# The first group's variances by adding transfers through DRAM, and x's first columns on SyncE's queue

## What is computed

```
def leaky_relu(x):
    return jnp.maximum(0.05 * x, x)

def layer_norm(x):
    mu = jnp.mean(x, axis=-1, keepdims=True)
    sigma = jnp.sqrt(jnp.mean((x - mu) ** 2, axis=-1, keepdims=True))
    return (x - mu) / sigma
x1, x2 = (x[:, :F], x[:, F:])
h1 = leaky_relu(layer_norm(x1 @ W1.T))      # W1: 256 x 5120
h2 = leaky_relu(layer_norm(x2 @ W1.T))
h1 = leaky_relu(layer_norm(h1 @ W2.T))      # W2: 64 x 256
h2 = leaky_relu(layer_norm(h2 @ W2.T))
h = jnp.concatenate([h1, h2], axis=-1)
h = leaky_relu(layer_norm(h @ W3.T))        # W3: 8 x 128
return h @ W4.T                             # W4: 1 x 8
```

## Time and profile before

| | |
|---|---|
| median of 3 runs | 234.36 us (234.24 to 234.99) |
| profiled execution | 234.42 us, of which the span of instructions is 232.6 us |
| PE busy | 226.7 us, 97% of the span |
| DVE, ACT busy | 191.1 us (82%), 151.9 us (65%) |
| POOL busy | 12.4 us (5%) |
| moved by DMA | 51.14 MB, 220 GB/s over the span |
| chain of work that ended last | 96% on PE, 91% in the large matmuls of L965 |

### The profile page before, as it was taken

The page is one execution under the profiler, slowest core; times in us unless marked ns, Lnnn a source line. Parts: engine busy times, 40 slices in busy tenths (PEclk is TensorE's granted clock), DMA queues, the critical chain, the costliest instruction groups (busy, mean ns, idle before and its releaser), DMA issues.

```text
span 232.6 us, 2919 instructions
## 1 busy us (share of the span) xinstructions
PE 226.7 (97%) x1022; PEld 183.8 (79%) x1022; DVE 191.1 (82%) x247; ACT 151.9 (65%) x240; POOL 12.4 (5%) x19
## 2 busy tenths in 40 slices
PE   7999999999999999999999999999999999999992
PEld 2788888888888888888878887888888888888772
DVE  3789999959789999895678499999989899949324
ACT  4897989689497598863775326636645677515630
POOL 0000020200200200000000410000000000000004
PEclk9999999999999999999999999999999999999996
DMA  6999999999899998446525526688675705050000
GB/s 203 394 408 409 400 322 318 319 244 346 293 246 388 254 308 323 150 158 249 204 100 205 194 92 194 232 275 285 205 266 209 233 1 180 16 164 4 0 0 1
DMA packets 17166, 51.14 MB, mean 220 GB/s; under 512 B 2176, under 2 KB 2560, under 8 KB 17152
## 3 DMA queue, kind: packets, MB, share of 16 engines
q1 hardware_dynamic: 15920, 48.60, 59.1%
q0 software_dynamic: 1088, 2.10, 5.2%
q10 hardware_dynamic: 144, 0.26, 0.3%
HBM read 50.95 MB, written 0.00 MB: 219 GB/s over the span
## 4 chain that ended last, share of the span: by engine, by line
PE 96%; DMA 1%; POOL 1%; DVE 1%; POOLq 0%; issue 0%; DVEq 0%
PE acc L965 91%; PE acc L1087 2%; PE acc L1100 2%; DMA stage<-w 1%; PE acc L1108 1%; POOL inv L473 0%; PE acc L1116 0%; POOLq L156 0%; POOL inv L478 0%; DVE w_mean L851 0%; DVE ws_hi L855 0%; DVE var L804 0%; DVE var L803 0%; DVE w_mean L853 0%; DVE y L829 0%
## 5 line engine op out<-in xcount | busy, mean ns | idle before, releaser
L549 ACT CAST xe_hi<-xe_raw 128x1024 fp32r<-128x1024 f32 (+1 forms) x48 | 48.2, 1011 | 32.6 <-PE acc L965 25.8
L965 PE MATMUL acc<-xe_lo,we_hi 128*128 128x512 f32 x176 | 68.8, 391 | 0.0
L965 PE MATMUL acc<-xe_hi,we_lo 128*128 128x512 f32 x176 | 68.6, 390 | 0.0
L665 DVE TENSOR_TENSOR xe_lo<-xe_raw,xe_hi 128x1024 fp32r<-128x1024 f32 (+1 forms) x48 | 55.5, 1177 | 13.8 <-ACT xe_hi L549 13.7
L965 PE MATMUL acc<-xe_hi,we_hi 128*128 128x512 f32 x176 | 48.2, 391 | 0.0
L965 PEld LDWEIGHTS acc<-xe_lo,we_hi 128*128 128x128 f32 x176 | 33.1, 188 | 7.5 <-issue 0.8
L965 PEld LDWEIGHTS acc<-xe_hi,we_lo 128*128 128x128 f32 x176 | 33.1, 188 | 6.7
L965 PEld LDWEIGHTS acc<-xe_hi,we_hi 128*128 128x128 f32 x176 | 33.0, 188 | 6.7
L549 ACT CAST xt_hi<-x_sum 128x2048 fp32r<-128x2048 f32 x14 | 26.8, 1912 | 16.1 <-DVE x_sum L736 16.1
L665 DVE TENSOR_TENSOR xt_lo<-x_sum,xt_hi 128x2048 fp32r<-128x2048 f32 x14 | 32.0, 2288 | 1.9 <-ACT xt_hi L549 1.9
L965 PE MATMUL acc<-xt_lo,ws_hi 128*128 128x512 f32 x64 | 25.1, 391 | 0.0
(11 more groups left out here) (102 smaller groups left out, 258.5 us busy)
## 6 DMA issues: line engine op xcount, KB each, us to landing
xe_raw<-x SPq DMA_DIRECT2D x51, 512.0 KB, 4.9
xs_raw<-x SPq DMA_DIRECT2D x14, 768.0 KB, 5.5
stage<-w SPq DMA_DIRECT2D x21, 256.0 KB, 5.7
x_sum<-x SPq DMA_DIRECT2D x10, 256.0 KB, 4.1
x_sum<-x SPq DMA_DIRECT2D x4, 512.0 KB, 4.4
x_sum<-x POOLq DMA_DIRECT2D x4, 512.0 KB, 8.8
xe_raw<-x ACTq DMA_DIRECT2D x1, 256.0 KB, 3.5
stage<-w SPq DMA_DIRECT2D x2, 128.0 KB, 3.4
```

The costliest lines, as they stand in the source:

```text
L549: act.copy(hi_of(u, part), raw_of(u, part)).then_inc(hi_ready[part.buffer], 1)
L665: dve.tensor_tensor(lo_of(u, part), raw_of(u, part), hi_of(u, part).bitcast(F32), ALU.subtract)\
L965: return pe.matmul(acc[:, bank, :], w, x, start=first, stop=True, skip_group_check=True)
```

## The change

**Transfers in place of matmuls.** For group 0 alone, TensorE no longer runs `sum_variance1` (8 instructions, 16 records) and `sum_variance2` (4 instructions, 8 records). POOL issues adding transfers (`accum_op=ADD`) instead: the squares of layer 1, in 128 partitions of 1024 numbers, are folded onto 64 partitions; then in six rounds the 64 rows of those and of the 2 x 64 of layer 2 are folded in halves onto one, two transfers a round, each round waiting for the one before. Three transfers store the resulting rows to DRAM, and six bring them back, turned, so that each partition gets its own numbers, in `var1` and `small`. That is 9 steps one behind the other, with 1 + 12 + 3 + 6 transfers.

**DVE.** The readout of both variances from PSUM goes. What needs them (`variance2`, `layer3`, `layer4`, `finish`) moves from the first S unit of group 1 to the sixth (`nth` 11), and there waits for `rows_landed`. The copy of layer 3's products stays where it was.

**SP.** The two weights that come again are loaded behind the fifth S unit of group 1 instead of the third, and wait for `rows_stored` too, since they go into the same part of `stage`.

**The start.** x's first 512 columns are issued second on SP's queue, not first on ACT's, and `WARM_UP` is 9.

**Bank P6.** TensorE's first use of it in group 1 waits for `drained` instead of `var1_copied`.

```
-WARM_UP = 8
+WARM_UP = 9
...
+        sq_rows = stage[:, 2 * NC:5 * NC]
+        sq1_rows, sq2_rows = sq_rows[:, 0:B * NC], sq_rows[:, B * NC:]
+        var1_rows = nc.dram_tensor("var1_rows", (B * NC,), F32, kind="Internal").ap()
+        var2_rows = nc.dram_tensor("var2_rows", (H, B * T * P), F32, kind="Internal").ap()
...
             sp.dma_start(w_raw[:, 0, 0:N1], w1[pair, :, 0:N1]).then_inc(first_w_landed, 16)
+            sp.dma_start(xe_raw[:, 0, 0:NC], first_half[:, 0:NC]).then_inc(first_x_landed, 16)
             sp.dma_start(xe_raw[:, 0, NC:], first_half[:, NC:]).then_inc(xe_landed[0], 16)
...
-                if n and n.n + 8 == W_WORK[len(FIRST)].n:
+                if n and n.n + 4 == W_WORK[len(FIRST)].n:
                     sp.wait_ge(h3_summed, B)
+                    sp.wait_ge(rows_stored, 16 * 3)
...
+            pool.wait_ge(sq1_summed, B)
+            pool.dma_start(sq1_rows[0:N2, :], sq1_rows[N2:, :], accum_op=ALU.add).then_inc(sq1_folded, 16)
+            pool.wait_ge(sq1_folded, 16)
+            pool.wait_ge(sq2_ready, B)
+            for k in range(6):
+                w = N2 >> (k + 1)
+                if k:
+                    pool.wait_ge(rows_folded, 32 * k)
+                pool.dma_start(sq_rows[0:w, :], sq_rows[w:2 * w, :], accum_op=ALU.add).then_inc(rows_folded, 16)
+                pool.dma_start(sq2_rows[N2:N2 + w, :], sq2_rows[N2 + w:N2 + 2 * w, :], accum_op=ALU.add)\
+                    .then_inc(rows_folded, 16)
+            pool.wait_ge(rows_folded, 32 * 6)
+            pool.dma_start(var1_rows.rearrange("(o n) -> o n", o=1), sq1_rows[0:1, :]).then_inc(rows_stored, 16)
+            for h in range(H):
+                pool.dma_start(var2_rows[h:h + 1, :], sq2_rows[h * N2:h * N2 + 1, :]).then_inc(rows_stored, 16)
+            pool.wait_ge(rows_stored, 16 * 3)
+            for b in range(B):
+                rows = var1_rows[(1 - b) * NC:(2 - b) * NC].rearrange("(h t p) -> t p h", h=H, t=T)
+                for t in range(T):
+                    pool.dma_start(var1[:, b * J + t * H:b * J + (t + 1) * H], rows[t],
+                                   allow_slow_non_contiguous=True).then_inc(rows_landed, 16)
+            for h in range(H):
+                pool.dma_start(small[:, h:B * J:H],
+                               var2_rows[h].rearrange("(k p) -> p k", p=P),
+                               allow_slow_non_contiguous=True).then_inc(rows_landed, 16)
...
-            act.dma_start(xe_raw[:, 0, 0:NC], x_half_of(0, u.pair, 0)[:, 0:NC]).then_inc(first_x_landed, 16)
...
                 if crosses(es):
-                    variance1(B, 0, B, var1_ps(0, 0, B))
                     dve.wait_ge(h3_summed, B)
-                    dve.wait_ge(var2_summed, B)
-                    dve.tensor_copy(small[:, 0:B * J], var2_ps(0, 0, B))
                     dve.tensor_copy(small[:, B * J:B * J + B * J * N3], h3_ps(0, 0, B)).then_inc(small_copied, 1)
+                first_end = n.nth == SEVEN + 5
+                if first_end:
+                    dve.wait_ge(rows_landed, 16 * (B * T + H))
+                    step(dve.reciprocal(var1_inverse[:], var1[:]))
                     dve.wait_ge(small_copied, 1)
                     variance2(B, 0, B, small[:, 0:B * J])
...
-                        pe.wait_ge(var1_copied, g)
+                        pe.wait_ge(drained, 5 * (g - 1) + 1)
...
-                    for b in range(B):
-                        sum_variance1(u.g - 1, b)
...
-                        sum_variance2(0, b)
```

More of the change, by code:

```diff
@@ L181, in rec_kernel @@
         sq1_sum = [h1[b][0] for b in range(B)]
+        sq_rows = stage[:, 2 * NC:5 * NC]
+        sq1_rows, sq2_rows = sq_rows[:, 0:B * NC], sq_rows[:, B * NC:]
+        var1_rows = nc.dram_tensor("var1_rows", (B * NC,), F32, kind="Internal").ap()
+        var2_rows = nc.dram_tensor("var2_rows", (H, B * T * P), F32, kind="Internal").ap()
         a2 = ([h1[b][1][:, 0:T * P] for b in range(B)], [xs_raw[:, 1, b * NC:b * NC + T * P] for b in range(B)])
-        sq2 = ([h1[b][1][:, T * P:] for b in range(B)], [xs_raw[:, 1, b * NC + T * P:(b + 1) * NC] for b in range(B)])
+        sq2 = ([sq2_rows[:, b * T * P:(b + 1) * T * P] for b in range(B)], [xs_raw[:, 1, b * NC + T * P:(b + 1) * NC] for b in range(B)])
         sq1_last = xs_raw[:, 0, 0:NC]
@@ L269, in rec_kernel @@
         var1_summed = sem("var1_summed")
+        sq1_folded = sem("sq1_folded")
+        rows_folded = sem("rows_folded")
+        rows_stored = sem("rows_stored")
+        rows_landed = sem("rows_landed")
         var2_summed = sem("var2_summed")
@@ L799, in variance1 @@
                 dve.tensor_copy(var1[:, a * J:b * J], summed).then_inc(var1_copied, 1)
-                dve.wait_ge(var1_copied, n - 1)
+                dve.wait_ge(var1_copied, n)
             def variance2(n, a, b, summed):
@@ L929, in _ @@
                 lo(after[0], after[0].parts[0])
-                if crosses(es):
+                if first_end:
                     layer3(1, 0, B, small[:, B * J:B * J + B * J * N3])
@@ L943, in _ @@
             sum_squares(g, 0)
-            variance1(B * g + 1, 0, 1, var1_ps(g, 0, 1))
+            variance1(1, 0, 1, var1_ps(g, 0, 1))
             sum_last_squares()
-            dve.wait_ge(var2_summed, B * g + 1)
+            dve.wait_ge(var2_summed, 1)
             variance2(2, 0, 1, var2_ps(g, 0, 1))
-            variance1(B * g + 2, 1, 2, var1_ps(g, 1, 2))
-            dve.wait_ge(var2_summed, B * g + 2)
+            variance1(2, 1, 2, var1_ps(g, 1, 2))
+            dve.wait_ge(var2_summed, 2)
             variance2(3, 1, 2, var2_ps(g, 1, 2))
```

## The result

| | median us | range, runs | ratio to the kernel before, 95% interval |
|---|---|---|---|
| before | 234.91 | 233.90 to 235.84, 9 | |
| changed kernel | 233.44 | 231.86 to 233.71, 9 | 0.9932 [0.9911, 0.9953] |
| changed kernel, second chip | 232.97 | 232.07 to 233.82, 7 | 0.9921 [0.9893, 0.9949] |

The change makes the kernel faster by 0.7 to 0.8%, 1.6 to 1.9 us. The forecast was 231.2 us, 3.2 us faster than the profiled execution before; the time lies above its range, 230.6 to 232.4. The profiled execution after took 233.68 us, with a span of 231.9 (before 234.42 and 232.6).

A forecast was written before the change was run, and what follows sets the result against it. TensorE, busy for 97% of the span, was taken as the bound. From the profiled 234.42 us, - 2.66 (matmuls) - 0.1 (old stall) - 0.6 (start) + 0.1 (new stall) gave 231.2 us, range 230.6 to 232.4.

The forecast's parts named there:

- matmuls leave TensorE, stall at 142.40 goes: Group 0's sum matmuls save 2.66 us of TensorE; a small stall in group 1 going saves 0.1 us.
- new stall before the product with `ws_lo`: At the norm's new place in group 1, TensorE waits 0.1 us more, bounds 0 and 1.0.
- start: At the kernel's beginning, the new load order and ninth matmul on zeros together gain 0.6 us, bounds -0.1 to 0.7.
- the transfers on POOL: Folding, stores and loads of the sums finish before DVE and SP ask: cost 0, margin 6 us, 4.8 us a step.
- What leaves TensorE: Sum matmuls near 120 to 128 us leave the chain: 2.66 us saved, bounds 2.5 to 2.7.
- can the others follow: Whether other engines deliver 2.66 us earlier: yes, as DVE saves 3.1 us in group 1; another 0.1 us gained.
- the one place at which the shift could be lost: DVE's work in group 1 up to `xt_lo`, without slack at 142.40 us, where a 2.66 us shift would be lost.
- The bound of -0.1: Worst case for the start and clock together: at most 0.1 us lost.
- the start gives nothing: Rival: x lands later and the clock rises as now, giving 231.8 us; chance 0.13.
- The clock: At the start, TensorE's clock may rise sooner with fewer early gaps; counted within the start's 0.6 us.
- Where the norm goes: Behind group 1's sixth S unit, DVE comes out 2.65 us later, cancelling the 2.66 us shift; stall 0.1 us.
- the 5.5 named as a sign of being wrong: For POOL's transfers, a folding step over 5.5 us would show the prediction wrong.

The follow-up runs named there:

- e2: The kernel before with both edits of the start (x's first 512 columns second on SP's queue, 9 matmuls on zeros): 235.20 us, ratio to before 1.0019.
- e7: The changed kernel with the old start, none of the 22 transfers (ones in place of sums), and the norm at its old place: 232.72 us, 0.992 of before.
- e6: The changed kernel itself, run and profiled again on a second chip: 232.97 us, 0.9921 of the kernel before.
- e13: The kernel of e12 with one more transfer, of 2 KB, second on SyncE's queue: 232.57 us, 0.9916 of the kernel before.
- e8: The changed kernel with the old start and none of the 22 transfers (ones in place of sums), norm at its new place: 232.06 us, 0.9892 of before.
- e9: The changed kernel with the old start, without the 9 stores and loads, keeping the 13 adding transfers: 233.54 us, one run, no ratio.
- e3: The kernel before with x's first 512 columns second on SP's queue, still 8 matmuls on zeros: 235.68 us, ratio to before 1.0033.
- e5: The changed kernel with the old start (x's first columns first on ACT's queue, 8 matmuls on zeros): 232.35 us, 0.9919 of the kernel before.
- e10: The changed kernel with the old start, without the 13 adding transfers, keeping the 9 stores and loads: 232.29 us, one run, no ratio.
- e4: The kernel before with 9 matmuls on zeros in place of 8, nothing else: 234.47 us, ratio to before 0.999.
- e12: The changed kernel with x's first columns back on ACT's queue, 9 matmuls on zeros, the norm one small unit earlier: 232.43 us, 0.9915 of before.
- e16: The same kernel as e12, run again for comparison on the same chip: 231.89 us, 0.9892 of the kernel before.

## Why the prediction was wrong

The sign was right, the size was not. Its terms, and what was measured:

| term of the sum | predicted, us | measured, us |
|---|---|---|
| matmuls leave TensorE, stall at 142.40 goes | -2.66 - 0.1 | -2.87 (layer 2 to layer 2, 101.12 to 98.25, where no new stall is) |
| new stall before the product with `ws_lo` | +0.1 | +0.35 (98.60 against 98.25; 0.25 of it a gap of TensorE) |
| start | -0.6 | +0.45 (e2; its interval allows -0.05 to +0.96) |
| the transfers on POOL | 0 | +0.33, at the end |
| sum | -3.26 | -1.7; timed -1.6 and -1.9 |

*What leaves TensorE* and *can the others follow* were right. The stretch from `xe_lo` on at 134.19, named as the one place at which the shift could be lost, was such a place: with the norm left there, 0.6 us are given back (e7). From layer 2 to layer 2 the changed kernel saves 2.5 us, where -2.66 - 0.1 + 0.1 was forecast; that the sign and this size came out is not luck.

*The start* is the step that failed, by 1.05 us: "If W1 lands 0.5 us earlier and x at the same time as now ... 0.5 us gained", and "So start and clock together give between -0.1 and 0.7; I take 0.6 us". In the first profile W1 came 1.1 us earlier, but x 1.0 us later. That is not what cost the gain: in e6 and e2, with the same order, W1 is used at 2.81 and 2.98 us, x at 3.72 and 3.85, and TensorE begins at 4.49 and 4.62, 0.6 and 0.5 us earlier than before, as much as was hoped for; and still layer 2 comes at 118.89 and 118.94, 0.8 us later than before. So the step that failed is the passage from the first product to the rest. It looked only at the two transfers it moved. It priced the issue "at 1.18 in place of 0.73" for x's first columns, and not for the seven loads queued behind them, which are issued 0.4 to 0.55 us later. It took the first product for what the start is about, where the third cast of x decides. The bound of -0.1 was wrong for the same reason. The rival "the start gives nothing" was nearer, but also without the loss. Why one issue of 0.47 us makes 0.7 to 0.8 us further on stays open.

The rule weighed there, in the Trainium skill, page "DMA: Bandwidth & Descriptors", section "Issuing engines are not separate DMA queues", says that a second issuing engine saves only the time of the issue, usually small beside the transfer. The runs agree with its first half: with two issuing queues kept, e13's one small transfer more makes the third cast as late as the changed kernel's. The second half misleads here: 0.47 us at the head of a row of loads is 0.7 us at the third cast.

*The clock.* Products with x one issue apart follow each other by 0.43 us at the 1.2 GHz level and by 0.23 at the 2.4 GHz level (the column of the granted clock reads 1.00 in every stretch of the start, so the level is read from the rows). In the changed kernel the rows at 7.06 and 7.30 us are at the higher one; before, it begins near 9.8 us. With nine products on zeros it begins by 7.3 us in all ten profiled executions; with eight, by 6.7 us in three (e7, e8, e9) and between 8.9 and 10.4 in four (before, e3, e5, e10). So the clock did rise sooner, as supposed. In time it brought nothing that can be told: e4 finds 0.999 [0.9969, 1.0011] for the ninth product alone. That TensorE then waits for casts of x (at 9.51 us in the changed kernel, for ACT) is a likely reason, not a shown one.

*Where the norm goes.* The mechanism was right and the size a bit off: DVE's wait for POOL is 1.57 us at 181.33, and `ws_lo` ends at 189.85, 1.5 us earlier than the 191.35 computed without the shift, as TensorE's need also moved. The stall was 0.25 us in place of 0.1, and one small unit earlier there is none (e12).

*The transfers on POOL.* A step was sized at 4.8 us and took 4.7; the rows were stored by 156.33 (forecast 155.5), though the first issue was 1.6 us late. The six loads took 4.4 us to issue instead of 9.6, and DVE asked at 178.02 for what had been issued by 160.76. So the cost inside the kernel is nothing, as said. One step, the second round of folding, took 7.1 us, over the 5.5 named as a sign of being wrong, without harm: it is the sum of the steps that counts, and there are 17 us between the last issue and DVE's question. The prediction put the end at nothing ("at the end the last norms do, which the change leaves alone"). That 22 transfers lengthen it by 0.33 us was in no row of before that the views print, and in no rival. By the Trainium skill, page "DMA: Bandwidth & Descriptors", section "Anatomy of one DMA — SWDGE (gpsimd) path", a step would have a fixed cost near 2.0 us; the steps here, beside other traffic, took 3.6 to 7.1 us, so the measurement decides and the rows of before were the better guide.

## What to carry to other kernels

A load moved onto an issuing queue delays the loads behind it by about its issue time, so list what follows it in that queue and ask which of those is waited for. Look at the first link of the chain that holds for long, not at the first product: where the compute engine must wait for the next pieces anyway, starting it earlier gives nothing. When small work is moved out of a tight stretch, try the neighbouring places too: one small unit earlier was worth 0.35 us of the traces here. Profile the same kernel twice before an order of landing at the start is explained: here x's first use was at 5.26 us in one execution and at 3.72 in the next.

## What the runs showed of the hardware

- GpSimd's closing DRAIN grows by 0.081 us with every transfer that GpSimd has issued: 1.15, 1.88, 2.21 and 2.94 us for 0, 9, 13 and 22 more. It counts as soon as it outlasts the landing of the last output: the end is 0.33 us longer with 22, and no longer with 9 or 13.
- At the start an issue on SyncE's queue mostly takes 0.47 us from one to the next, for 2 KB (e13, 1.15 to 1.62) as for 512 KB (x's half at 2.56 to 3.04).
- With W1 and then x in one queue, W1 is used at 2.81 to 2.98 us and x at 3.72, 3.85, 5.26 and 6.15 (e6, e2, changed, e3); with one on each of two queues (before, e4, e5, e7 to e10, e12, e16), W1 at 3.73 to 4.11 and x at 4.02 to 4.34. What makes x scatter by 2.4 us in one queue stays open.
- The landing of the same load at the start scatters by over 1 us between executions of like kernels (third cast 6.90 to 8.53 us), and layer 2 begins at 117.64 to 119.76 us. From there to `y` kernels of one layout agree within 0.1 us (before and e4 112.5 us; e12 to e16 109.6), so most of what makes two runs of this kernel differ lies at the start.
